# One transfer for each expert's weights, asked for after the second layer, in a two-block vision tower

## The reference

```
h = patches(x) @ W + b                                # 512 tokens, width 192
h = h + linear_attention(layernorm(h))                # 12 heads, random features
h = h + moe32(layernorm(h))                           # the part that is changed
h = h + softmax_attention_with_rope(layernorm(h))
h = h + moe8_plus_shared(layernorm(h))

# moe32: 4 groups of 8 experts; the best 2 groups, the best 2 experts in each
h1 = gelu(einsum('nd,edm->nem', xf, W1) + b1)         # 192 -> 768
y  = einsum('nem,emd->ned', h1, W2) + b2              # 768 -> 192
out = einsum('ne,ned->nd', comb, y)                   # comb: 4 non-zero weights a token
```

## Time and profile before

| | us |
|---|---|
| median of 3 runs | 298.04 (296.31 to 300.12) |
| the profiled execution, its own time | 298.84 |
| its span, first to last instruction | 297.0 |
| TensorE busy | 276.7 (93%) |
| VectorE / ScalarE / GpSimd busy | 150.7 / 112.6 / 58.3 |
| moved by the DMA engines | 70.69 MB |

### The profile page before, as it was taken

One profiled execution on the slowest core, in us unless ns is written; L12 is line 12 of the kernel. 1 busy time (PEld: TensorE's weight loads), 2 busy tenths in 40 slices (PEclk: granted clock), 3 DMA queues, 4 the chain that ended last, 5 costly groups with the idle time before them and its releaser, 6 DMA issues.

```text
span 297.0 us, 7516 instructions
## 1 busy us (share of the span) xinstructions
PE 276.7 (93%) x2670; PEld 182.6 (61%) x2670; DVE 150.7 (51%) x422; ACT 112.6 (38%) x387; POOL 58.3 (20%) x73
## 2 busy tenths in 40 slices
PE   8989999799999999999999999976989889999993
PEld 6957877565565665665665565554966777355543
DVE  0465685783655544445644633300428864574444
ACT  1156251333336436346335435450162756211100
POOL 5600000022244244244243332120200000000000
PEclk9999999997999999999999999997899999899999
DMA  7993009968799999999999999815910000000001
GB/s 267 388 412 123 4 2 324 386 198 324 272 407 410 405 406 408 405 407 410 405 409 406 406 402 405 351 43 206 402 64 0 4 3 0 0 0 2 0 0 53
DMA packets 19864, 70.69 MB, mean 238 GB/s; under 512 B 3584, under 2 KB 4805, under 8 KB 19696
## 3 DMA queue, kind: packets, MB, share of 16 engines
q1 hardware_dynamic: 17328, 65.62, 56.7%
q0 software_dynamic: 2208, 3.43, 3.3%
q10 hardware_dynamic: 288, 1.13, 1.0%
HBM read 68.71 MB, written 3.28 MB: 242 GB/s over the span
## 4 chain that ended last, share of the span: by engine, by line
PE 76%; DVE 11%; DMA 7%; issue 3%; ACT 1%; SPq 1%; DVEq 1%; ACTq 0%; POOLq 0%
PE ps L1015 15%; PE ps L972 11%; PE ps L977 6%; PE ps L1082 6%; PE ps L991 6%; PE ps L1094 4%; PE ps L1085 3%; DMA attn_rows<-in_attn_rows 3%; PE ps L1052 2%; DMA x_rows<-xn_rows,row_ids 2%; PE ps L951 2%; PE ps L754 2%; DMA y_picks<-fexp,row_ids 2%; PE ps L943 1%; PE ps L774 1%
## 5 line engine op out<-in xcount | busy, mean ns | idle before, releaser
L657 ACT ACTIVATE turned<-ps,route_in 128x64 f32<-128x64 f32 x288 | 61.4, 340 | 70.1 <-PE ps L991 70.0
L508 POOL DMA_INDIRECT x_rows<-xn_rows,row_ids x22 | 23.0, 1044 | 112.0 <-DVE row_ids L1290 57.4
L1305 DVE COPY probs<-ps 128x768 f32<-128x768 f32 x24 | 22.9, 956 | 22.9 <-PE ps L977 22.9
L520 POOL DMA_INDIRECT y_picks<-fexp,row_ids x24 | 24.3, 1011 | 26.6 <-DVE fexp L1398 16.7
L1015 PE MATMUL ps<-late_in,turned 128*64 128x192 f32 x216 | 26.0, 329 | 1.2 <-ACT turned L657 1.2
L1015 PE MATMUL ps<-expert_w,turned 128*64 128x192 f32 x288 | 25.8, 329 | 0.0
L1015 PEld LDWEIGHTS ps<-late_in,turned 128*64 128x64 f32 x216 | 19.0, 137 | 5.0 <-ACT turned L657 1.8
L1015 PEld LDWEIGHTS ps<-expert_w,turned 128*64 128x64 f32 x288 | 19.3, 137 | 4.4 <-ACT turned L657 1.2
L1398 DVE COPY fexp<-ps 128x192 f32<-128x192 f32 x24 | 8.6, 357 | 25.1 <-PE ps L1015 25.1
L991 PE MATMUL ps<-cst,probs 128*128 128x128 f32 x144 | 21.1, 281 | 0.2 <-DVE fexp L1300 0.2
L972 PE MATMUL ps<-late_in,fexp 128*64 128x384 f32 x72 | 19.4, 539 | 0.2 <-issue 0.2
(11 more groups left out here) (245 smaller groups left out, 456.0 us busy)
## 6 DMA issues: line engine op xcount, KB each, us to landing
expert_w<-in_experts SPq DMA_DIRECT2D x48, 576.0 KB
late_in<-in_experts SPq DMA_DIRECT2D x36, 576.0 KB, 10.0
probs<-in_experts SPq DMA_DIRECT2D x12, 576.0 KB, 11.9
late_in<-in_ffn_in SPq DMA_DIRECT2D x1, 2592.0 KB, 11.7
probsT<-in_patches SPq DMA_DIRECT2D x4, 384.0 KB, 7.0
qk_padT<-y_picks SPq DMA_DIRECT2D x4, 384.0 KB, 4.6
late_in<-in_attn_in SPq DMA_DIRECT2D x1, 864.0 KB, 5.7
attn_w<-in_attn_w SPq DMA_DIRECT2D x1, 673.5 KB, 8.9
```

Of the source, the lines that this page charges most:

```text
L508: pool.indirect_dma_start(out=x_rows[:, x_u, :], out_offset=None, in_=xn_rows, in_offset=bass.IndirectOffsetOnAxis(ap=row_ids[:, u % STEPS ...
L520: pool.indirect_dma_start(out=y_picks, out_offset=bass.IndirectOffsetOnAxis(ap=row_ids[:, u, 1:2], axis=0), in_=y_rows[:, u % RING, :], in ...
L657: last = act.activation(hidden[:, u % 2, half * (KH // 2) + c, slots_of(q)], ps[:, 4 + half, c * P + q * SLOTS:c * P + (q + 1) * SLOTS], A ...
L1305: dve.tensor_copy(raw.rearrange("p (h n) -> p h n", h=2), ps[:, 2:4, 0:HID // 2]).then_inc(raw_sb, 1)
```

## The change

The two halves of an expert's weights come in one transfer of 128 rows of 9216 bytes (1152 KB) in place of two of 4608-byte rows. Both are asked for where the second half was: when the second layer of tile u is done, the whole pair of tile u + 4. The request for the first half of tile u + 5 behind the first layer of tile u + 1 is gone, and so is the one for tile 4 behind the first layer of tile 0. One semaphore for each slot (w_dma) stands for both halves; `up_in` waits for it, and the second layer no longer waits for a transfer.

```diff
-            def load_pair(i, ov_round, u, cols, done):
+            def load_pair(i, ov_round, u):
                 for q in range(PAIR):
                     e = expert_of(sp, i, ov_round, u, q)
-                    sp.dma_start(weights[u % RING * PAIR + q][:, cols], dram["experts"][bass.ds(e, 1), :, cols].rearrange("a p n -> (a p) n")).then_inc(done[u % RING], 16)
+                    sp.dma_start(weights[u % RING * PAIR + q], dram["experts"][bass.ds(e, 1), :, :].rearrange("a p n -> (a p) n")).then_inc(w_dma[u % RING], 16)
...
             for u in range(RING // 2, RING):
-                load_first(0, None, u)
-                load_second(0, None, u)
-            sp.wait_ge(up_mm, 1)
-            load_first(0, None, RING)
+                load_pair(0, None, u)
...
                     with where_tile(sp, tiles, ov_round, u):
-                        with where_tile(sp, tiles, ov_round, u + 1 + RING):
-                            sp.wait_ge(up_mm, i * STEPS + u + 2)
-                            load_first(i, ov_round, u + 1 + RING)
                         with where_tile(sp, tiles, ov_round, u + RING):
                             sp.wait_ge(down_mm, i * STEPS + u + 1)
-                            load_second(i, ov_round, u + RING)
+                            load_pair(i, ov_round, u + RING)
...
-                pe.wait_ge(w1_dma[u % RING], 16 * PAIR * (i * (STEPS // RING) + u // RING + 1))
+                pe.wait_ge(w_dma[u % RING], 16 * PAIR * (i * (STEPS // RING) + u // RING + 1))
...
-                        pe.wait_ge(w2_dma[u % RING], 16 * PAIR * (i * (STEPS // RING) + u // RING + 1))
```

More of the change, by code:

```diff
@@ L353, in vit_tower @@
         pick_diag_ready, picks_mm = sem("pick_diag_ready"), sem("picks_mm")
-        w1_dma, w2_dma, x_dma, y_dma = ([sem(f"{n}{u}") for u in range(RING)] for n in ("w1_dma", "w2_dma", "x_dma", "y_dma"))
+        w_dma, x_dma, y_dma = ([sem(f"{n}{u}") for u in range(RING)] for n in ("w_dma", "x_dma", "y_dma"))
         rowsT_mm, rowsT_sb, up_mm, raw_sb, rawT_mm, gelu_done, down_mm, y_ready = (
```

## The result

The changed kernel takes 304.83 us (median of 4 runs, 300.84 to 307.82) against 298.21 (4 runs, 296.31 to 300.12) for the kernel before on the same chip: a ratio of 1.0178, interval 1.0115 to 1.0241. The medians are of all runs and the ratios with their intervals of the fast runs alone (within 1.5% of the kernel's fastest), so the two can differ: on the second chip the quotient of the medians is 1.020. The two intervals meet at 1.022 to 1.024; the forecast of 305.0 over 298.04 is 1.023.

A forecast was written before the change was run, and what follows sets the result against it. Weight DMA was taken as the slower resource, with TensorE living on its lead; later requests and whole-tile waits, less long-row gains, lengthen the stage by 6.2 us: 298.84 + 6.2 = 305.0, range 300 to 314 for 8 in 10.

The forecast's parts named there:

- Two resources full, the lead nearly used up: Expert stage: DMA at 6.31 us a tile, TensorE at 5.60, its lead down to 1.6 us at tile 23.
- there is nothing else to give: TensorE idles under 1 us from 130 to 185; even with weights never late the time is 297.
- Last landing = 77.2 + 1.9 + 19 x T: Tile 23's weights: request time, latency, 19 whole tiles of DMA time T; at 6.15 it lands at 196.0, stage +6.2 us.
- The cost of a row: Weight transfers: 17 ns fixed per row, 345 ns for 9216 bytes against 362 for two short rows, giving T = 6.03.
- the 440 GB/s stretch: Last big load's 20,736-byte rows, against 407; gives T's lower bound 5.84, doubted as a short window.
- The idle stretch around 73 to 77: DMA engines idle until tile 5's request at 77.18; some 0.55 of a tile, 3.5 us, lost to later requests.
- The wait for a whole tile: First layer of tile 23 needs both halves: 6.3 us more, less 1.6 of lead; 8.2 with the 3.5 of later requests.
- Where waits begin: TensorE waits of 0.3 to 0.7 us a tile before the first layer from tile 11 to 13 on, none before tile 10.
- Gathers bind: Rival: token gathers beside long rows become the stage's bound; 308 to 320 us, middle 315, chance 0.27.
- The doubling of the 3.5 us: If a gather waits behind a number of rows, twice the row length doubles its loss: 7.25 us a tile.
- Long rows pay: Rival: weight rows near T = 5.84, deciding from 5.9 or less, rate above 425 GB/s; 297 to 302 us, chance 0.18.
- Faster: Rival: over 2% faster, held not to be had in this stage; chance 0.03.

The follow-up runs named there:

- e4: Changed kernel, but from tile 8 on only the first-layer half of the weight columns is moved; 295.72 us, 0.9859 of the kernel before.
- e5: Kernel before with each half in two transfers of 2304-byte rows, asked for and waited for as before; 308.75 us, ratio 1.0311.
- e3: Changed kernel's later requests and wait for both halves, but in separate half transfers of 4608-byte rows; 307.13 us, 1.0240 of the kernel before.
- e1: Kernel before with both halves asked for behind the second layer, each half keeping its own transfers and wait; 304.12 us, ratio 1.0187.
- e2: Kernel before with the first layer waiting for both halves, requests and rows unchanged; 305.75 us, ratio 1.0211.
- e9: Changed kernel measured again without edit, on another chip beside the kernel before; 305.90 us against 299.79, ratio 1.0289.
- e8: Kernel before with 9216-byte rows for home tiles, one layer's half for both experts per transfer, requests and waits unchanged; 301.02 us, ratio 1.0106.
- e7: Changed kernel with tile 4 loaded ahead into two more buffers, so tile 8 is asked for behind tile 0; 301.99 us, 1.0116 of the kernel before.

## Why the prediction was right

The sign, the mechanism and the size held: 305.0 was forecast, 304.83 and 305.90 were measured, within 300 to 314. That the first profile's stage came to within 0.05 us of the forecast is luck: the second is 2.1 longer, and some terms below missed by more. Point by point:

*Two resources full, the lead nearly used up.* Right, and e4 shows it directly: with the DMA engines relieved TensorE is never idle and the stage is shorter than before. Wrong in one point: "there is nothing else to give" (under 1 us). e4's stage is 1.7 us shorter than the kernel before's and its time 1.4% lower.

*Last landing = 77.2 + 1.9 + 19 x T.* T was 6.15 by choice. Tile 6's last transfer, asked for at 82.2, lands 9.1 later:

```profile
L419 SPq DMA_DIRECT2D late_in<-in_experts x2: 327/380/434, 81.9 to 82.2; - x2
DMA to landing us min/median/max: 5.5/7.3/9.1
```

That is 91.3, and tile 23 lands at 194.92: T = (194.92 - 91.3) / 17 = 6.10. With it the formula gives 195.0. First layer of tile 23 at 195.15, forecast 196.0; stage +6.25, forecast +6.2.

*The cost of a row.* A row took 4608 x 16 / 407 = 181 ns before and takes 9216 x 16 / 415 = 355 now; in e5 it is 2304 x 16 / 389 = 94.8. The three lie on a line with some 7 to 8 ns of fixed cost, not the 17 that I had drawn through the 440 GB/s stretch. Transfers grow with their rows in all these kernels, so the runs don't tell a fixed cost of a row from one of a transfer. So the 2% of rate that long rows bring are right for T (6.31 x 407 / 415 = 6.19, and 6.10 measured), and the doubt put on the 440 was well placed.

*The idle stretch around 73 to 77.* The total was right, its place and the sign given for it were wrong. I had forecast 50 to 100 GB/s there; it shows 238, and the hole is in slice 9. Tile 4's and tile 5's requests:

```profile
L419 SPq DMA_DIRECT2D expert_w<-in_experts x2: 327/380/433, 67.5 to 67.8; - x2
DMA to landing us min/median/max: 5.1/7.0/8.8
...
L419 SPq DMA_DIRECT2D expert_w<-in_experts x2: 328/380/433, 75.8 to 76.2; - x2
```

Tile 5 is asked for at 75.8, since this kernel runs 0.8 us ahead here and not at 77.18; tile 4 lands at 67.8 + 8.8 = 76.6, not 75.5. So the queue runs nearly dry for a moment only (DMA share 0.70). The missing half tile is in the 60 to 67 before, where the kernel before already had requests for the first halves, tile 4's from 59.2 on; the prediction had counted that one into 65 to 77. Two errors that cancelled in the sum, which is luck. What the idle time costs in all, put at 3.5 us, is 4.0 by e3 and 4.4 by e1.

*The wait for a whole tile.* Right in kind (6.3 less the 1.6 of lead); e3, which has the changed timing without the long rows, shows the sum of both parts: +8.9 against 8.2 and 9.2. What I had not seen is how the parts overlap: either of them alone, e1 or e2, already costs 6 to 7 us. The DMA engines finish at nearly the same time in both kernels, the last weights having moved by 193.8 before and 194.0 after (195.8 in e9); from the start of the stage that is 110.2, 111.2 and 113.2 us, against 114.2 in e3. So later requests cost 4.0 us and long rows give 3.0 back, in e9 1.0. What the time is lost to is that before, the last 6.3 us of transfers lay under work, and now nothing of them does.

*Where waits begin.* Forecast tile 11 to 13, 0.3 to 0.7 us a tile. The first is at tile 13 (timeline of TensorE, with the wait in brackets):

```profile
134.84 1.51 PE L959 MATMUL ps<-expert_w,fexp 128*64 128x384 f32 x8 [0.40 <-DMA expert_w<-in_experts]
```

0.40 us here, 6.10 - 5.60 = 0.50 a tile over the stage. In e9 they begin at tile 10.

*Gathers bind (0.27).* No; in the changed kernel they hold PE up for 0.6 us and PEld for 1.8, of which the pace of the weights leaves little to see in the time. The doubling of the 3.5 us did not come: all gathers of the changed kernel, and of e3 with its short rows at the same timing:

```profile
DMA to landing us min/median/max: 2.7/6.6/7.2
```

```profile
DMA to landing us min/median/max: 4.8/5.7/6.3
```

The first fence is of the changed kernel, the second of e3. The median rises by 0.6 from the kernel before's 6.0, or by 0.9 from e3's 5.7. The rule of the Trainium skill that I had weighed ("DMA: Bandwidth & Descriptors", the section on queues, rings and completion order: a turn drains a whole packet of descriptors) would have doubled the gather's share of waiting; the rows show a rise of a sixth to a quarter of it. Still the rise exists, and e8 is the kernel in which it shows.

*Long rows pay (0.18).* No: it needed T at 5.9 and over 425 GB/s; 6.10 and 415 were measured. The Trainium skill's rule on batching to 1 MiB ("DMA: Bandwidth & Descriptors", section Bandwidth), with its formula for one DMA, would have had nearly a third off T, an estimate (by the formula 1152 KB run at 251 GB/s, not the 249 that I had). The page measured both on transfers issued from GpSimd, and these are SyncE's. The trace does not agree: from 576 to 1152 KB the rate rose by 2%, from 288 to 576 KB (e5) by 5%. With several requests always in the queue, size matters little in these runs.

*Faster, and the change not doing what it says.* Neither came.

What stays open: a pause of 0.44 us in front of the first layer of tile 9 (at 111.66, with nothing that the profile shows to wait for), which e7 and e8, the other kernels with 9216-byte rows, show at the same tile with 0.39 and 0.43, and e9 at tile 8 with 0.38; and how much of the 2.1 us between the two profiles of the changed kernel is the chip's.

## What to carry to other kernels

When two resources are both full, ask which lives on the other's lead, and follow the last landing: a merge of two transfers costs, at the end of the stream, the time of everything that used to stand behind the first of them in the queue, even though the DMA engines finish no later. Splitting a buffer's release and its arrival by who uses which half was worth 6 to 7 us of a stage of 112 here for either part alone, and loading one tile ahead gave back 2 to 4 of them. Measure the stage, from a fixed instruction to a fixed instruction: the part behind it moved by 3.5 us here for reasons that lie elsewhere. And take more than one profile: the stage itself moved by 2.1.

## What the runs showed of the hardware

- With requests always queued, the rate depends little on the size of a transfer: 389, 407 and 415 GB/s with rows of 2304, 4608 and 9216 bytes (transfers of 288, 576 and 1152 KB), gathers included.
- A gather by GpSimd beside the full stream lands in 5.7 to 6.6 us (median of one profile each: e3, before, changed) where it takes 2.9 alone, and doubling the stream's rows adds 0.6 to 0.9.
- Requests cost SyncE 0.33 us each, and with eight a tile and a table read for each overflow expert they become the bound (e5).
- The same matmuls behind the stage took 592 ns in the median and up to 1222 in the same execution. At a mean granted clock of 0.94 in place of 0.98 there, TensorE was busy for 2.8 us more.
